# The last up product of a two-layer Flamingo block in three fp32r passes

## The chip, the cores and the metric

The kernel is one program on one core of a Trainium2 chip. The metric is device time in microseconds (us), the median of three timed runs; the rows below come from one further execution that the hardware profiler recorded. TensorE is PE, VectorE is DVE, ScalarE is ACT, GpSimd is POOL, and SP issues DMAs. Each engine works its own queue in order; engines meet only through semaphores.

## What is computed

Two layers over `x` of 16 sequences x 128 rows x 128, each layer a cross attention to a context and a feed-forward part. Layer 0 has 16 heads and a mixture of 16 experts (four chosen per row); layer 1 has one head and a feed-forward part whose hidden size is 512, with butterfly transforms on both sides of the gelu:

```
x = x + tanh(g_xattn[0]) * xattn0(layernorm(x), ctx)
x = x + tanh(g_ffn[0])   * mixture(layernorm(x))
x = x + tanh(g_xattn[1]) * xattn1(layernorm(x), ctx)
x = x + tanh(g_ffn[1])   * ffn1(layernorm(x))
# ffn1
h = einsum('bsd,dh->bsh', x, W_exp) + b_exp
h = butterfly(h, up_weights, 512)
h = gelu(h + up_bias)
h = butterfly(h, down_weights, 512)
y = einsum('bsh,hd->bsd', h, W_con) + b_con + down_bias
```

A butterfly is linear, so the kernel multiplies its 9 stages into the weights once: `W_exp` with the up stages gives `wup` (128 x 512), `W_con` with the down stages gives `wdn`. What is left of `ffn1` per row is an up product with `wup`, a gelu and a down product with `wdn`.

## The kernel before

All engines run one hand-written order; no scheduler decides anything. The 16 sequences go in four groups `g` of 512 rows.

**First 155 us: layer 0's attention.** PE, ACT and DVE work on scores, exponentials and sums. Meanwhile POOL splits the expert weights into a rounded fp32r part and a remainder (L387, L388), then runs the 18 butterfly stages of the weights in `stage` (L424 on). A stage is two 128x512 multiplies (L365, L369), one addition (L373) and a fetch of the next coefficients (L339). Stage 8 (`k == STAGES - 1`) writes `wup`; stages 9 to 17 make the down weights in `bfly`. Between stages POOL has other duties in a fixed place: after stage 9 the second norm of the first half and `norm_rows(0)` (L469, L471), which PE turns at L923 with `turn_normed(0)`; after stage 15 `remainders(0)` (L484), which PE's first expert product waits for. After stage 17 come the up bias, `values1` (L422), `norm2(1)`, and then POOL's `mixture(0)`, whose first piece is `router_ties(1)` (L503, L504). DVE's `router_chosen(1)` (L1301 on) waits for those ties, DVE's next expert work is queued behind it, and PE's `turn_gates(1)` (L937) waits for DVE's gates.

**155 to 350 us: the mixture.** `up(g, e)` is already in the split form: three passes for each of two branches (L994, L995, L996), fp32r, 512 columns. `down(g, e - 3)` is one full fp32 product (L1005). Layer 1's attention of group `g - 1` is strewn among the experts of group `g`. PE is the engine the others wait for in most of it.

**From 350 us: layer 1's feed-forward.** PE turns the normed rows of a group (`turn_rows`, L1028); ACT's `hidden_xt` (L762) copies them from PSUM to `xnts`, and signals `d_xnt`. PE's `hidden_in(g, c)` (L1113) is one full fp32 product for each of four 128-wide slices `c` of the hidden size, ACT's `hidden` (L767) the gelu, and PE's `hidden_out` (L1128) the down product; group 3 is done in half groups (`hidden_half`, L1120 and L773). For group 0 the four `hidden_in` stand between the last three `down` products of the mixture; then `turn_rows(1)` and `turn_mixed(3)` (L1017). DVE's order here is: the last two experts (L1434, L1437, L1442), `attn1_stats(2)` (L1402, L1405), `variances` (L1185 to L1193), `residual2(3)` (L1350, L1353), the statistics and norms of layer 1's attention for group 3 (`attn1_norm`, L1376), `normed(2)` (L1417), and so on to `residual4` (L1425).

`high(g)` and `low(g)` are the two fp32r halves of slot `g % 2` of `xhl`, the tile that holds the mixture's split rows.

Of the kernel before, what the change touches and what calls it, by code (L numbers as in the profile page):

```python
# [7 lines left out]
F32 = mybir.dt.float32  # L8
# [32 lines left out]
def flamingo_layers(nc, a, out):  # L41
# [20 lines left out]
    with ExitStack() as ctx:  # L62
        def sb(name, shape, dt=F32):
            return ctx.enter_context(nc.sbuf_tensor(name, shape, dt))
# [96 lines left out]
        bfx = sb("bfx", [P, HID])  # L161
        ubs = sb("ubs", [HC, 3, P])
        ubx = sb("ubx", [P, 3, HC])
        ubw = sb("ubw", [HC, (STAGES - 2) * 2 * P])
        wup = sb("wup", [P, HID])
        wdn = sb("wdn", [P, HC, D])
        upb = sb("upb", [P, HC])
        kt_flat = kt_row[:, :, :].rearrange("p g t -> p (g t)")
        xns = (xn, rings[:, 0, 1, :].rearrange("p (b d) -> p b d", b=GB))
        xnts = (xnt[:, :], rings[:, 0, 0, :])  # L170
        hid = ([bw[:, c // 2, c % 2 * GT:(c % 2 + 1) * GT] for c in range(HC)],
               [qt_row[:, 0, :], qt_row[:, 1, :], kt_flat[:, 0:GT], kt_flat[:, GT:2 * GT]])
        bcd = sb("bcd", [P, D])
# [10 lines left out]
        def turned_bank(b, gg):  # L184
# [8 lines left out]
            w1_split b1_rdy  # L193
            m_xn m_turned m_xnt m_xh m_xl m_lg_mm m_lgd m_exp m_gf m_g_turned gt_st m_gt m_ha m_hb m_gate0 m_gate1 m_gate2 m_gate3 m_sg m_eb m_eq
            m_ec m_s m_y m_ys m_ys_turned m_x2 c_xn c_turned c_xnt c_q c_qt c_s c_max c_exp c_p_turned c_pt c_pv c_x3
            ln2_var ln2_pow x1_st c_st c_rs x3_st d_rs m_xo m_cmp m_ties d_xn d_bias d_turned d_xnt d_h d_g d_o d_x4 d_out dve_own pool_own bw_ld0 bw_ld1 
            bf_rdy wd_turned wd_rdy us_rdy ub_turned ub_rdy upb_rdy""".split()
        s = {n: sem(n) for n in names}

        CH = (SB[1], SB[3], PQ, SB[2], PO)  # L200
# [6 lines left out]
        def pipelined(eng, body):  # L207

            for g in range(G):
                body(g)  # L210
# [18 lines left out]
        def _(sp):  # L229
# [11 lines left out]
            sp.dma_start(rows[:, :], bass.AP(tensor=v.tensor, offset=v.offset, ap=[[0, P], [1, v.shape[0]]])  # L241
                         ).then_inc(s["ld_small"], 16)
            sp.dma_start(ubs[:, 0, :], a["L1_ffn_b_exp"]).then_inc(s["ld_ub"], 16)
            sp.dma_start(ubw[:, :], a["flies_chunks"]).then_inc(s["ld_ub"], 16)

            def stack_k(g):
                for i in range(HG):
# [63 lines left out]
        def _(pool):  # L311
# [16 lines left out]
            def fetch(n):  # L328

                if n < NQ:  # L330
                    src = a["L0_ffn_w1"][:, 4 * n:4 * n + 4, :, :]
                    dst = bw[:, n % 2, :].rearrange("p (e t c) -> p e t c", e=4, t=2)
                elif n < NQ + 2 * STAGES:
                    v = a["flies"]
                    src = bass.AP(tensor=v.tensor, offset=v.offset + (n - NQ) * 2 * HID, ap=[[0, P], [1, 2 * HID]])
                    dst = bw[:, n % 2, :]
                else:
                    return
                pool.dma_start(dst, src).then_inc(s[f"bw_ld{n % 2}"], 16)  # L339
# [86 lines left out]
            def stage(k, op):  # L426

                n = NQ + k
                w, down = bw[:, n % 2, :], k >= STAGES
                S = 2 ** (2 * STAGES - 1 - k if down else k)  # L430
                if k == STAGES:
                    src = wdn[:, :, :].rearrange("p c d -> p (c d)")
                else:
                    src = bfly[:, (k - STAGES if down else k) % 2, :]
                dst = wup[:, :] if k == STAGES - 1 else bfly[:, ((k - STAGES if down else k) + 1) % 2, :]
                if op == 0:
                    fetched(n)
                    straight(bft[:, :], w[:, 0:HID], src)
                if op == 1:
                    crossed(bfx[:, :], w[:, HID:2 * HID], src, S, HID)  # L440
                if op == 2:
                    summed(dst, bft[:, :], bfx[:, :])
                    fetch(n + 2)

            def norm_scales(stat, mean_, scales, n, both=False):

# [117 lines left out]
        def _(act):  # L564
# [194 lines left out]

            def hidden_xt(g):  # L760
                act.wait_ge(s["d_turned"], g + 1)
                act.activation(xnts[g % 2], (TP if g == 0 else PK)[:, :], ACT.Copy).then_inc(s["d_xnt"], 1)  # L762

            def hidden(g, c):
                need(act, "d_o", g - 1)
# [35 lines left out]
        def _(pe):  # L801
# [305 lines left out]
                        down(g - 1, E - LAG + e)  # L1107

            pipelined(pe, mixture)
            def hidden_in(g, c):  # L1110
                pe.wait_ge(s["d_xnt"], g + 1)
                need(pe, "d_g", g * HC + c - 4)
                pe.matmul(CH[(g * HC + c) % 5][:, :], wup[:, c * P:(c + 1) * P], xnts[g % 2], start=True,  # L1113
                          stop=True).then_inc(s["d_h"], 1)

            def hidden_half(c, i):
                g, t = G - 1, slice(i * GT // 2, (i + 1) * GT // 2)
                pe.wait_ge(s["d_xnt"], g + 1)
                need(pe, "d_g", (g + i) * HC + c - 4)
                pe.matmul(CH[((g + i) * HC + c) % 5][:, t], wup[:, c * P:(c + 1) * P], xnts[g % 2][:, t], start=True,  # L1120
                          stop=True).then_inc(s["d_h"], 1)

            def hidden_out(g, us):
                pe.wait_ge(s["d_g"], (g + 1) * HC + (HC if g == G - 1 and 3 in us else 0))
# [6 lines left out]
                    mm.then_inc(s["d_o"], 1)  # L1131

            every = range(GB)
            pe.wait_ge(s["m_sg"], G * E - 1)
            hidden_in(0, 0)
            down(G - 1, E - 3)
# [37 lines left out]
        def _(dve):  # L1174
# [7 lines left out]
            def variances(n, stat, mean_, both=False, at=0):  # L1182

                c = slice(at, at + n)
                own.mark(dve.tensor_tensor(mean_, stat[:, :, 1], stat[:, :, 4], ALU.add))  # L1185
                own.mark(dve.tensor_tensor(cs[:, 2, 0, c], stat[:, :, 1], stat[:, :, 4], ALU.subtract))
                own.mark(dve.tensor_tensor(cs[:, 3, 0, c], stat[:, :, 2], stat[:, :, 5], ALU.add))
                own.wait()
                own.mark(dve.tensor_scalar(mean_, mean_, 0.5, None, ALU.mult))
                own.mark(dve.tensor_tensor(cs[:, 2, 0, c], cs[:, 2, 0, c], cs[:, 2, 0, c], ALU.mult))  # L1190
                own.mark(dve.tensor_scalar(cs[:, 3, 0, c], cs[:, 3, 0, c], 1.0 / D, EPS, ALU.mult, ALU.add))
                own.wait()
                ins = dve.scalar_tensor_tensor(cs[:, 0, 0, c], cs[:, 2, 0, c], 0.25, cs[:, 3, 0, c],  # L1193
                                               ALU.mult, ALU.add)
                if both:
                    own.then_wait(ins)
                    ins = dve.tensor_scalar(cs[:, 0, 1, c], cs[:, 0, 0, c], 1.0 + EPS, -EPS, ALU.mult, ALU.add)
                ins.then_inc(s["ln2_var"], 1)
# [181 lines left out]
            def attn1_maxima(g):  # L1380
                dve.wait_ge(s["c_s"], g + 1)
                dve.tensor_reduce(mx1[:, :], TP[:, 0:GB * M].rearrange("p (b m) -> p b m", b=GB),
                                  AX.X, ALU.max, negate=True).then_inc(s["c_max"], 1)
# [185 lines left out]
```

## Time and profile before

| | |
|---|---|
| timed runs | 389.17, 392.10, 392.59 us; median 392.1 |
| profiled execution | 395.04 us, of which the span is 393.1 |
| mean granted TensorE clock | 0.912 of full speed |
| PE busy | 324.5 us (83%), 2600 instructions |
| DVE busy | 257.4 us (65%), 602 |
| ACT busy | 209.6 us (53%), 405 |
| POOL busy | 206.9 us (53%), 270 |

Times in the rows are from the span's start. "Busy" is a sum over instructions and says nothing of who waits for whom; that is read from the chain of what ended last and, at each place, from the rows of the engines in order of time. A matmul's printed duration contains its way through the array: what it costs its successors is the distance between starts. A full fp32 product appears as two instructions (x2).

### The profile page before, as it was taken

The page shows a single profiled execution, that of the slowest core. Times are in us where ns is not written, and L with a number is a line of the kernel's source. Part 1 is how long each engine was busy: PE and PEld are TensorE (multiplying, and loading weights), DVE is VectorE, ACT ScalarE, POOL GpSimd, SP SyncE. Part 2 cuts the span into 40 slices and gives each one's busy share as a digit, 9 for nine tenths or more (in the row PEclk, how much of TensorE's full clock was granted, in tenths as well). Part 3 has the DMA queues.
Part 4 walks back from the last instruction along what each step waited for, and adds up shares of the span by engine and source line. Part 5 has one row for each costly group of instructions (what it writes and reads, how often), then busy time and mean ns, then how long its engine had stood idle before and what let it go on. Part 6 is the DMA issues. An engine that isn't in the chain of part 4 may idle for free.

```text
span 393.1 us, 7226 instructions
## 1 busy us (share of the span) xinstructions
PE 324.5 (83%) x2600; PEld 228.2 (58%) x2600; DVE 257.4 (65%) x602; ACT 209.6 (53%) x405; POOL 206.9 (53%) x270
## 2 busy tenths in 40 slices
PE   5758689698799912899199998799998999899986
PEld 2435567576577811666066665566655666555866
DVE  8531436556466287398868789697896887795450
ACT  2642146466366610567145584765866746855543
POOL 7463899979598999999600193002900059122120
PEclk9996759989899755699779999999999999999999
DMA  7669222645531233333133222232322433100001
GB/s 245 129 142 120 86 63 107 133 131 120 112 110 59 69 123 116 128 106 105 29 104 116 80 91 72 85 119 67 105 87 80 119 95 108 53 0 1 28 28 55
DMA packets 17235, 36.66 MB, mean 93 GB/s; under 512 B 2384, under 2 KB 4068, under 8 KB 17064
## 3 DMA queue, kind: packets, MB, share of 16 engines
q1 hardware_dynamic: 13184, 23.53, 21.2%
q0 software_dynamic: 3168, 11.54, 10.8%
q10 hardware_dynamic: 848, 1.14, 0.9%
q8 instruction: 21, 0.34, 0.4%
q14 instruction: 14, 0.11, 0.1%
HBM read 32.79 MB, written 1.18 MB: 86 GB/s over the span
## 4 chain that ended last, share of the span: by engine, by line
PE 36%; POOL 32%; DMA 11%; DVE 7%; issue 6%; ACT 6%; SPq 1%; ACTq 0%; DVEq 0%; POOLq 0%
PE bank L1005 9%; POOL bft L365 6%; POOL bfx L369 5%; POOL bfly L373 5%; PE bank L996 5%; PE bank L994 4%; PE bank L995 4%; DMA bw<-in_L_ffn_w 4%; DMA bw<-in_flies 4%; PE bank L1128 4%; PE bank L1113 3%; DMA x_sb<-in_x 3%; POOL bw L339 2%; POOL w_lo L388 2%; POOL v_all L422 2%
## 5 line engine op out<-in xcount | busy, mean ns | idle before, releaser
L994 PE MATMUL bank<-xhl,w_hi 128*128 128x512 f32 x128 | 76.3, 596 | 0.5 <-ACT rings L734 0.5
L734 ACT ACTIVATE rings<-bank,cols 128x512 f32<-128x512 f32 x64 | 44.1, 689 | 60.9 <-PE bank L996 50.1
L1245 DVE TENSOR_REDUCE nt<-bank 128x4 f32<-128x480 f32 x64 | 39.9, 650 | 46.2 <-PE bank L878 46.2
L1434 DVE SCALAR_TENSOR_TENSOR rings<-rings,gates 128x512 f32<-128x512 f32 x64 | 47.9, 749 | 20.9 <-ACT rings L734 20.5
L996 PE MATMUL bank<-xhl,w_hi 128*128 128x512 f32 x128 | 51.6, 403 | 0.0
L995 PE MATMUL bank<-xhl,w_lo 128*128 128x512 f32 x128 | 51.5, 402 | 0.0
L871 PE MATMUL bank<-rings,ks 32*120 32x128 f32 x512 | 41.7, 306 | 11.4 <-DMA rings<-mxr 6.2
L878 PE MATMUL bank<-ks,rings 32*128 32x120 f32 x512 | 42.9, 312 | 5.8 <-DMA rings<-qt_row 4.0
L871 PEld LDWEIGHTS bank<-rings,ks 32*120 32x120 f32 x512 | 35.2, 201 | 17.4 <-DMA rings<-mxr 8.5
L738 ACT ACTIVATE rings<-bank,b1c 128x512 f32<-128x512 f32 x64 | 44.0, 688 | 1.0 <-PE bank L996 0.6
L878 PEld LDWEIGHTS bank<-ks,rings 32*128 32x128 f32 x512 | 36.5, 213 | 6.6 <-issue 4.2
L994 PEld LDWEIGHTS bank<-xhl,w_hi 128*128 128x128 f32 x128 | 24.8, 194 | 18.8 <-issue 8.4
L995 PEld LDWEIGHTS bank<-xhl,w_lo 128*128 128x128 f32 x128 | 24.9, 194 | 17.5 <-issue 14.4
L484 POOL TENSOR_TENSOR xhl<-xnt,xhl 128x512 fp32r<-128x512 f32 x4 | 5.1, 1270 | 55.5 <-ACT xhl L660 55.4
L1005 PE MATMUL bank<-wide,x_sb 128*128 128x512 f32 x64 | 33.6, 607 | 0.0
L1005 PE MATMUL bank<-rings,x_sb 128*128 128x512 f32 x64 | 33.3, 602 | 0.0
L1437 DVE TENSOR_SCALAR rings<-rings 128x512 f32<-128x512 f32 x64 | 28.9, 452 | 0.7 <-ACT rings L738 0.6
L996 PEld LDWEIGHTS bank<-xhl,w_hi 128*128 128x128 f32 x128 | 24.7, 193 | 5.9
L1442 DVE TENSOR_TENSOR wide<-rings 128x512 f32<-128x512 f32 x32 | 24.0, 749 | 4.2
L1442 DVE TENSOR_TENSOR rings<-rings 128x512 f32<-128x512 f32 x32 | 23.0, 719 | 4.6 <-DVE rings L1437 0.5
L365 POOL TENSOR_TENSOR bft<-bw,bfly 128x512 f32<-128x512 f32 x17 | 21.6, 1272 | 5.4 <-DMA bw<-in_flies 5.1
L937 PE MATMUL bank<-ident,gf 128*16 128x128 f32 x16 | 3.3, 342 | 25.1 <-DVE gf L1315 25.1
(227 smaller groups left out, 688.1 us busy)
## 6 DMA issues: line engine op xcount, KB each, us to landing
gates<-gate_rows SPq DMA_DIRECT2D x64, 256.0 KB, 3.1
bw<-in_flies POOLq DMA_DIRECT2D x18, 512.0 KB, 4.3
bw<-in_L_ffn_w POOLq DMA_DIRECT2D x4, 512.0 KB, 7.8
x_sb<-in_x SPq DMA_DIRECT2D x4, 256.0 KB, 8.3
x_sb<-in_L_ffn_w SPq DMA_DIRECT2D x1, 1024.0 KB, 4.9
wide<-in_ctx ACTq DMA_DIRECT2D x4, 240.0 KB, 7.2
ks<-kt_row SPq DMA_DIRECT2D x16, 60.0 KB
out<-xr SPq DMA_DIRECT2D x3, 256.0 KB, 2.4
```

Of the source, the lines that this page charges most:

```text
L365: own.mark(pool.tensor_tensor(dst, w, src, ALU.mult))
L734: act.activation(esg[:, e % 2, :], SB[1 + e % 2][:, :], ACT.Gelu_apprx_sigmoid, bias=b1_in[:, 0, e:e + 1]).then_inc(s["m_sg"], 1)
L738: act.activation(eb[:, e % 2, :], (SB[3], PK)[e % 2][:, :], ACT.Identity, bias=b1c[:, e:e + 1]).then_inc(s["m_eb"], 1)
L871: mm = pe.matmul(turned_bank(b, gg)[0:M, r * P:(r + 1) * P], ks[32 * gg:32 * gg + 32, i, r, mc], qs[32 * gg:32 * gg + 32, i, r, tc], start ...
L878: mm = pe.matmul(score_bank(ahead, n)[:, r * M:(r + 1) * M], qs[rows32, ia, r, ta], ks[rows32, ia, r, ma], start=True, stop=True)
L994: pe.matmul(bk[:, :], w1_hi[:, e, branch, :], low(g), start=True, stop=False)
L995: pe.matmul(bk[:, :], w1_lo[:, e, branch, :], high(g), start=False, stop=False)
L996: pe.matmul(bk[:, :], w1_hi[:, e, branch, :], high(g), start=False, stop=True).then_inc(s[done], 1)
L1005: pe.matmul(Y[:, :], w2_sb[:, e, :], es[e % len(es)], start=False, stop=(e == E - 1), skip_group_check=True).then_inc(s["m_y"], 1)
L1245: dve.tensor_reduce(nt[:, b % 2, OF[n], :], score_bank(b, n)[:, 0:HR * M].rearrange("p (r m) -> p r m", r=HR), AX.X, ALU.max, negate=True) ...
L1434: dve.scalar_tensor_tensor(eq[:, j, :], esg[:, j, :], GELU_LIMIT, gates[:, (n - 1) % NG, :], ALU.min, ALU.mult).then_inc(s["m_eq"], 1)
L1442: dve.tensor_tensor(es[e % len(es)], eq[:, j, :], ec[:, j, :], ALU.mult).then_inc(s["m_s"], 1)
```

## The change

The up product of `ffn1` takes the form that the mixture's up product has: weights and rows are each split into a rounded fp32r part and a remainder, and three fp32r passes (remainder of the weights by rounded rows, rounded by rounded, rounded by remainder of the rows) add up in PSUM.

```diff
-        ubw = sb("ubw", [HC, (STAGES - 2) * 2 * P])
-        wup = sb("wup", [P, HID])
+        ubw = gates[0:HC, :, :].rearrange("p n t -> p (n t)")[:, 0:(STAGES - 2) * 2 * P]
+        wup_hi = sb("wup_hi", [P, HID], F32R)
+        wup_lo = sb("wup_lo", [P, HID], F32R)
@@ stage (POOL)
-                dst = wup[:, :] if k == STAGES - 1 else bfly[:, ((k - STAGES if down else k) + 1) % 2, :]
+                dst = bfly[:, ((k - STAGES if down else k) + 1) % 2, :]
                 if op == 2:
                     summed(dst, bft[:, :], bfx[:, :])
                     fetch(n + 2)
+                    if k == STAGES - 1:
+                        own.then_wait(pool.tensor_copy(wup_hi[:, :], dst))
+                        pool.tensor_tensor(wup_lo[:, :], dst, wup_hi[:, :].bitcast(F32), ALU.subtract).then_inc(s["wup_rdy"], 1)
+                        pool.wait_ge(s["wup_rdy"], 1)
@@ hidden_xt (ACT)
-                act.activation(xnts[g % 2], (TP if g == 0 else PK)[:, :], ACT.Copy).then_inc(s["d_xnt"], 1)
+                act.activation(high(g), (TP if g == 0 else PK)[:, :], ACT.Copy).then_inc(s["d_xh"], 1)
@@ PE
+            def hidden_product(bk, g, c, t):
+                w = slice(c * P, (c + 1) * P)
+                pe.wait_ge(s["d_xh"], g + 1)
+                pe.matmul(bk[:, t], wup_lo[:, w], high(g)[:, t], start=True, stop=False)
+                pe.matmul(bk[:, t], wup_hi[:, w], high(g)[:, t], start=False, stop=False)
+                pe.wait_ge(s["d_xnt"], g + 1)
+                pe.matmul(bk[:, t], wup_hi[:, w], low(g)[:, t], start=False, stop=True).then_inc(s["d_h"], 1)
@@ DVE
+            def hidden_remainder(g):
+                dve.wait_ge(s["d_xh"], g + 1)
+                dve.tensor_tensor(low(g), (TP if g == 0 else PK)[:, :], high(g).bitcast(F32), ALU.subtract
+                                  ).then_inc(s["d_xnt"], 1)
+
             variances(GB, stats[:, two:three, :], mean[:, two:three], at=GB)
+            hidden_remainder(0)
+            hidden_remainder(1)
             residual2(G - 1)
@@
             residual4(0, every)
+            hidden_remainder(2)
             attn1_maxima(G - 1)
@@
             residual4(2, every)
+            hidden_remainder(3)
             residual4(3, every[:2])
```

`hidden_in` and `hidden_half` call `hidden_product` where they had one matmul. So `d_xnt`, which ACT signalled, is now DVE's signal, and ACT's is `d_xh`. PE also waits once for `wup_rdy` before the tail. `ubw`, the coefficients of the bias stages, now lies in the `gates` tile, which is idle until the mixture.

The order of the instructions, at the places that move. POOL, from stage 8's two multiplies to stage 9's (before):

```order
L365 TENSOR_TENSOR bft<-bw,bfly 128x512
L369 TENSOR_TENSOR bfx<-bw,bfly 128x512
L373 TENSOR_TENSOR wup<-bft,bfx 128x512
L339 DMA bw<-in_flies 128x1024
L365 TENSOR_TENSOR bft<-bw,wdn 128x512
```

and now:

```order
L365 TENSOR_TENSOR bft<-bw,bfly 128x512
L369 TENSOR_TENSOR bfx<-bw,bfly 128x512
L373 TENSOR_TENSOR bfly<-bft,bfx 128x512
L339 DMA bw<-in_flies 128x1024
L445 CAST wup_hi<-bfly 128x512
L446 TENSOR_TENSOR wup_lo<-bfly,wup_hi 128x512
L365 TENSOR_TENSOR bft<-bw,wdn 128x512
```

Two instructions stand in POOL's queue ahead of stage 9 and all that follows it. DVE, from the last expert to `residual2(3)`, before (`cs`, `stats`, `mean` are the variances' tiles):

```order
L1434 SCALAR_TENSOR_TENSOR rings<-rings,gates 128x512
L1437 TENSOR_SCALAR rings<-rings 128x512
L1442 TENSOR_TENSOR wide<-rings 128x512
L1402 COPY gs<-tg 128x1
L1405 BN_STATS stats<-xr 128x6 x4
L1185 TENSOR_TENSOR mean<-stats 128x4
...
L1193 SCALAR_TENSOR_TENSOR cs<-cs 128x4
L1350 TENSOR_TENSOR wide<-wide,bank 128x512
L1353 SCALAR_TENSOR_TENSOR xr<-wide,tg,xr 128x512
```

and now:

```order
L1443 SCALAR_TENSOR_TENSOR rings<-rings,gates 128x512
L1446 TENSOR_SCALAR rings<-rings 128x512
L1451 TENSOR_TENSOR wide<-rings 128x512
L1411 COPY gs<-tg 128x1
L1414 BN_STATS stats<-xr 128x6 x4
L1194 TENSOR_TENSOR mean<-stats 128x4
...
L1202 SCALAR_TENSOR_TENSOR cs<-cs 128x4
L1488 TENSOR_TENSOR xhl<-bank,xhl 128x512 x2
L1359 TENSOR_TENSOR wide<-wide,bank 128x512
L1362 SCALAR_TENSOR_TENSOR xr<-wide,tg,xr 128x512
```

The remainders of groups 0 and 1 stand behind the last expert, the statistics and the variances, and ahead of `residual2(3)`. PE at the end of the mixture, before (L1028 is `turn_rows`, L1005 `down`, L1113 `hidden_in`):

```order
L1028 MATMUL bank<-ident,xn 128x128 x4
L1005 MATMUL bank<-rings,x_sb 128x512
L1113 MATMUL bank<-xnt,wup 128x512
L1005 MATMUL bank<-rings,x_sb 128x512
L1113 MATMUL bank<-xnt,wup 128x512
L1005 MATMUL bank<-wide,x_sb 128x512
```

and now:

```order
L1028 MATMUL bank<-ident,xn 128x128 x4
L1005 MATMUL bank<-rings,x_sb 128x512
L1117 MATMUL bank<-xhl,wup_lo 128x512
L1118 MATMUL bank<-xhl,wup_hi 128x512
L1120 MATMUL bank<-xhl,wup_hi 128x512
L1005 MATMUL bank<-rings,x_sb 128x512
L1117 MATMUL bank<-xhl,wup_lo 128x512
```

Each L1113 row (two instructions on the chip) has become three, of which the last (L1120) waits for DVE, with the mixture's remaining `down` products queued behind it.

## Rows read from the trace of the kernel before

**Rows 1.** The page's chain that ended last: shares of the span by engine
```profile
PE 36%; POOL 32%; DMA 11%; DVE 7%; issue 6%; ACT 6%; SPq 1%; ACTq 0%; DVEq 0%; POOLq 0%
```

**Rows 2.** POOL in order of time: start, duration (us), engine, line, operation, tiles, count, [idle before <-releaser]
```profile
44.60 1.05 POOL L387 CAST w_hi<-bw 128x1024 fp32r<-128x1024 f32 x1
45.73 2.33 POOL L388 TENSOR_TENSOR w_lo<-bw,w_hi 128x1024 fp32r<-128x1024 f32 x1
...
113.32 1.28 POOL L365 TENSOR_TENSOR bft<-bw,wdn 128x512 f32<-128x512 f32 x1
...
125.70 1.04 POOL L471 TENSOR_TENSOR xn<-xn,rr 128x512 f32<-128x512 f32 x1
...
155.25 1.28 POOL L484 TENSOR_TENSOR xhl<-xnt,xhl 128x512 fp32r<-128x512 f32 x1
...
187.57 0.25 POOL L504 TENSOR_TENSOR gw<-gw 128x32 f32<-128x32 f32 x1
```

**Rows 3.** PE in order of time, up to the restart of the mixture
```profile
127.56 0.60 PE L923 MATMUL bank<-ident,xn 128*128 128x128 f32 x4
...
159.90 0.78 PE L994 MATMUL bank<-xhl,w_hi 128*128 128x512 f32 x1
...
186.67 0.40 PE L995 MATMUL bank<-xhl,w_lo 128*128 128x512 f32 x1
186.91 0.40 PE L996 MATMUL bank<-xhl,w_hi 128*128 128x512 f32 x1
195.64 1.02 PE L937 MATMUL bank<-ident,gf 128*16 128x128 f32 x4 [8.34 <-DVE gf L1315]
```

**Rows 4.** DVE in order of time: the router's wait, then the tail
```profile
187.86 0.22 DVE L1301 TENSOR_REDUCE gs<-gw 128x4 f32<-128x64 f32 x1 [2.36 <-POOL gw L504]
...
351.58 0.69 DVE L1442 TENSOR_TENSOR wide<-rings 128x512 f32<-128x512 f32 x1
...
354.03 0.16 DVE L1193 SCALAR_TENSOR_TENSOR cs<-cs 128x4 f32<-128x4 f32 x1
357.56 0.69 DVE L1350 TENSOR_TENSOR wide<-wide,bank 128x512 f32<-128x512 f32 x1 [3.36 <-PE bank L1017]
...
363.98 1.11 DVE L1417 TENSOR_SCALAR xn<-xr,mean,rr 128x128 f32<-128x128 f32 x4
```

**Rows 5.** PE in order of time, in the tail
```profile
350.30 1.10 PE L1113 MATMUL bank<-xnt,wup 128*128 128x512 f32 x2
351.24 1.02 PE L1005 MATMUL bank<-rings,x_sb 128*128 128x512 f32 x2
352.09 1.02 PE L1113 MATMUL bank<-xnt,wup 128*128 128x512 f32 x2
...
356.82 0.60 PE L1017 MATMUL bank<-ident,wide 128*128 128x128 f32 x4
357.76 3.67 PE L1113 MATMUL bank<-rings,wup 128*128 128x512 f32 x8 [0.34 <-ACT rings L762]
...
366.13 1.12 PE L1047 MATMUL bank<-rings,wt 128*128 128x512 f32 x2 [0.25 <-ACT rings L705]
...
382.82 3.72 PE L1120 MATMUL bank<-rings,wup 128*128 128x256 f32 x16 [0.69 <-ACT rings L762]
```

**Rows 6.** ACT in order of time, in the tail
```profile
349.56 0.60 ACT L762 ACTIVATE xnt<-bank 128x512 f32<-128x512 f32 x1 [0.34 <-PE bank L1028]
...
377.12 0.69 ACT L767 ACTIVATE bw<-bank,upb 128x512 f32<-128x512 f32 x1 [0.46 <-PE bank L1113]
```

**Rows 7.** Windows of 1 us: length, busy us of PE, PEld, DVE, ACT, POOL, clock, DMA share, GB/s
```profile
190.00:191.00 1.00, 0.00 (x0) 0.00 (x0) 0.97 (x2) 0.00 (x0) 0.92 (x2) 0.87 0.00 0
191.00:192.00 1.00, 0.00 (x0) 0.00 (x0) 0.96 (x2) 0.00 (x0) 1.00 (x2) 0.50 0.00 0
...
200.00:201.00 1.00, 1.00 (x4) 0.81 (x3) 0.59 (x1) 0.41 (x2) 0.00 (x0) 0.51 0.32 94
201.00:202.00 1.00, 1.00 (x4) 0.47 (x4) 0.41 (x2) 1.00 (x2) 0.00 (x0) 1.00 0.00 0
```

More of the change, by code:

```diff
@@ L169, in flamingo_layers @@
         xns = (xn, rings[:, 0, 1, :].rearrange("p (b d) -> p b d", b=GB))
-        xnts = (xnt[:, :], rings[:, 0, 0, :])
         hid = ([bw[:, c // 2, c % 2 * GT:(c % 2 + 1) * GT] for c in range(HC)],
@@ L195, in flamingo_layers @@
             m_ec m_s m_y m_ys m_ys_turned m_x2 c_xn c_turned c_xnt c_q c_qt c_s c_max c_exp c_p_turned c_pt c_pv c_x3
-            ln2_var ln2_pow x1_st c_st c_rs x3_st d_rs m_xo m_cmp m_ties d_xn d_bias d_turned d_xnt d_h d_g d_o d_x4 d_out dve_own pool_own bw_ld0 bw_ld1
-            bf_rdy wd_turned wd_rdy us_rdy ub_turned ub_rdy upb_rdy""".split()
+            ln2_var ln2_pow x1_st c_st c_rs x3_st d_rs m_xo m_cmp m_ties d_xn d_bias d_turned d_xh d_xnt d_h d_g d_o d_x4 d_out dve_own pool_own bw_ld0 bw_ld1
+            bf_rdy wup_rdy wd_turned wd_rdy us_rdy ub_turned ub_rdy upb_rdy""".split()
         s = {n: sem(n) for n in names}
@@ L243, in _ @@
             sp.dma_start(ubs[:, 0, :], a["L1_ffn_b_exp"]).then_inc(s["ld_ub"], 16)
-            sp.dma_start(ubw[:, :], a["flies_chunks"]).then_inc(s["ld_ub"], 16)
+            sp.dma_start(ubw, a["flies_chunks"]).then_inc(s["ld_ub"], 16)
             def stack_k(g):
@@ L1109, in _ @@
             pipelined(pe, mixture)
+            def hidden_product(bk, g, c, t):
[5 more added lines that the diff above has]
+                pe.matmul(bk[:, t], wup_hi[:, w], low(g)[:, t], start=False, stop=True).then_inc(s["d_h"], 1)
             def hidden_in(g, c):
-                pe.wait_ge(s["d_xnt"], g + 1)
                 need(pe, "d_g", g * HC + c - 4)
-                pe.matmul(CH[(g * HC + c) % 5][:, :], wup[:, c * P:(c + 1) * P], xnts[g % 2], start=True,
-                          stop=True).then_inc(s["d_h"], 1)
+                hidden_product(CH[(g * HC + c) % 5], g, c, slice(0, GT))
             def hidden_half(c, i):
-                g, t = G - 1, slice(i * GT // 2, (i + 1) * GT // 2)
-                pe.wait_ge(s["d_xnt"], g + 1)
+                g = G - 1
                 need(pe, "d_g", (g + i) * HC + c - 4)
-                pe.matmul(CH[((g + i) * HC + c) % 5][:, t], wup[:, c * P:(c + 1) * P], xnts[g % 2][:, t], start=True,
-                          stop=True).then_inc(s["d_h"], 1)
+                hidden_product(CH[((g + i) * HC + c) % 5], g, c, slice(i * GT // 2, (i + 1) * GT // 2))
             def hidden_out(g, us):
@@ L1133, in _ @@
             every = range(GB)
+            pe.wait_ge(s["wup_rdy"], 1)
             pe.wait_ge(s["m_sg"], G * E - 1)
```

## The prediction

> **What bounds the kernel now.** I read the chain that ended last first, because the table of busy shares would mislead: PE is busy 83% of the span, yet the chain is 36% PE and 32% POOL [rows 1]. So POOL, with 53% busy, holds a third of the end time. Then I read each engine in order of time at the two places that the change touches.
>
> The first is POOL's long run. It works without a gap from stage 8 of the butterflies to the ties of the router, whose last piece starts at 187.57. DVE had waited 2.36 us for that piece, and PE, whose last expert pass before it started at 186.91, stood still 8.34 us until 195.64, when DVE's gates came [rows 2 to 4]. Whatever is added to POOL's queue ahead of 187.57 arrives at PE at 195.64. From there on the expert products follow each other on PE almost without idle time, so the delay reaches the end.
>
> The second is the tail from 350 us. There PE goes through `hidden_in` and `down` back to back [rows 5], ACT has its gelus, and DVE is at first late: it finishes the last expert only at 352.2 (351.58 and 0.69) and the variances at 354.03 and 0.16 [rows 4].
>
> **The change part by part.**
>
> *Weights on POOL.* Two instructions are added. For 1024 columns the rounding took 1.05 and the subtraction 2.33 [rows 2]. For 512 columns the same kind of subtraction took 1.28, so 2.33 = fixed + 2 x (1.28 - fixed) gives a fixed part of 0.23. With it the rounding of 512 columns is 0.23 + 0.82/2 = 0.64. Each instruction is followed by a wait on POOL's own semaphore of about 0.08 (45.65 to 45.73). Sum: 0.64 + 1.28 + 0.16 = **2.1 us**, bounded by 0.53 for a rounding of exactly half and 1.05 for one as long as the row: 2.0 to 2.5. The stage's own addition stays, with another target. The fetch is issued before the split, so no transfer gets later. All the rest of POOL's queue moves by 2.1. What waits for it earlier than 187.57? PE turns `xn` at 127.56, and POOL had written it by 126.74 [rows 2, 3]: now 128.8, so PE stops for about 1.3 there. The first expert pass at 159.90 needs the remainder that ended at 156.53; now 158.6, still early. The 1.3 is hidden, since DVE has 2.36 + 2.1 to spare at the ties. So 2.1 goes through to PE's restart.
>
> *The products themselves.* One fp32r pass costs 0.24 (186.67 to 186.91; six passes and a down product fill 2.25 in the mixture), three cost 0.70. A full fp32 product costs 0.86 (351.24 to 352.09) [rows 3, 5]. So 0.16 is saved for each of 12 full-width products, and for the eight half ones, 3.72/8 = 0.465 now, some 0.345 is my estimate (three times 0.115, half a pass), saving 0.12 each. Total at most 12 x 0.16 + 8 x 0.12 = 2.9, if PE sets the end at each.
>
> The Trainium skill (FP8 and Floating Point Precision, section TensorE Precision Notes) counts four passes for true fp32, and TensorE: Matmul & The Clock Gate (section "Wait — 56ns, not 53.3ns?") a full-speed pace of 215.7 ns for 512 columns: four passes against three would save 0.216 a product. That would be 2.6 instead of 1.9 for the twelve, 0.7 us better than my sum. The rows give fp32r passes 0.233 to 0.24 apart, and I go by the rows.
>
> *Rows on ACT.* `hidden_xt` writes `high(g)` instead of `xnts`, the same copy of 512 columns (0.60) [rows 6]. Nothing.
>
> *Rows on DVE: the new wait.* The subtraction reads PSUM and has 512 columns, like the 0.69 of L1350 [rows 4]. For group 0 ACT's copy is ready at 349.56 + 0.60 = 350.16, but DVE reaches the remainder only behind the last expert, the statistics and the variances, at 354.1, and ends it at 354.8. PE used to begin `hidden_in(0, 0)` at 350.30. It now does two passes by 350.77 and then stands until about 354.9; the third ends at 355.15 where the full product had made way at 351.24. **PE is 3.95 late**. Nothing on DVE depends on what is queued behind the third pass until `residual2`, so this is a wait and no deadlock. Queued behind it are three `down` products, `hidden_in(0, 1..3)`, `turn_rows(1)` and `turn_mixed(3)`. Three more `hidden_in` at 0.16 less make `turn_mixed` start at 360.3 instead of 356.82: 3.5 late.
>
> DVE then would begin `residual2` 0.74 after that, at 361.05. But ahead of it stands the remainder of group 1. ACT copies that group's rows after `turn_rows(1)`, from 360.55 to 361.15; the remainder runs 361.2 to 361.9. So `residual2`, 357.56 before, starts at 361.9: **4.35 late**. All of `residual2`, the statistics, `attn1_norm` and `normed(2)` follow it by 4.35. `normed(2)`, which ended at 365.09 (363.98 + 1.11), ends at 369.45 [rows 4]. PE meanwhile: `hidden_in(1)` from 361.3, its first third pass held 0.25 by DVE, four products until 364.4, `hidden_out(0)` until 367.9; it then waits for `attn1_norm` (368.4) and `normed(2)` (369.45). Its chain to `attn1_q`, 366.13 before, waits for ACT's copy and then for the turned rows: it starts at 369.95, **3.8 late** [rows 5]. From there to the softmax of group 3 the order of before repeats, shifted 3.8.
>
> *What comes back.* Group 2's `hidden_in` ends earlier: its last three products save 0.48, and the first lets ACT load its gelu table 0.16 sooner. The last gelu, at 377.12 before after 0.46 of waiting for PE [rows 6], starts about 0.65 sooner. In group 3 the half products start when ACT has copied (382.82 before [rows 5]); the remainder holds the first third pass until 0.78 later, and eight products save 8 x 0.12 = 0.96. With the two passes done meanwhile (0.23), that is 0.25 better. Together 0.9 back.
>
> *Sum for the tail*: 3.8 - 0.9 = **2.9 late**, although PE's own work got shorter. Sum of all: 2.1 + 2.9 = **5.0**. The profiled execution's span of 393.1 becomes 398.1, and its time 395.04 becomes 400.0. It stood 2.9 above the median of the timed runs, 392.1; the same step puts the median at **397.1**.
>
> **The rivals.**
>
> *The clock falls in the new stall (chance 0.25).* In the pause from 187.3 the granted clock went from full, 2.4 GHz, to half, 1.2 GHz, at about 190.9, 3.6 after PE's last work, and was back only at 201.0, 5.4 after PE began again [rows 3, 7]. The new stall is 4.1 us long (350.8 to 354.9), a little more than 3.6. If the clock falls there too and stays for 5.4, the 5.4 hold half the work: 2.7 more, with part of it off the path, so some 2.5. Time: 399.6. It decides if the clock is still at full when the third pass starts. Against it: pauses of 1 to 1.6 us in the mixture left it at full. The Trainium skill warns of just this (TensorE: Matmul & The Clock Gate, section "HAM oscillation — how this bites in real kernels": idle gaps put the clock back down).
>
> *One of the two terms is hidden (0.17).* If POOL's 2.1 were taken up, by DVE or PE work that turns out to bound at 187, or if the restart and half-speed stretch at 195.6 end sooner relative to the restart, only the tail counts: 395.0. If DVE reaches its remainders sooner, or the attention of group 3 has more give than the rows show, the sum is 394 to 395.5. Both are within 1% of before.
>
> *The gain wins (0.06), the other sign.* The mechanism: PE's work in the tail is what ends last, and DVE's remainder comes while PE would be busy anyway. Then 2.9 are gained; with POOL's 2.1 the time is 391.3, and 389.2 if that too is hidden. It needs DVE to deliver group 0's remainder before 350.8; the rows have DVE in the last experts until 352.2 and the remainder behind nine more instructions, which speaks against it. It decides from the point where that third pass waits less than 0.5.
>
> **How the numbers follow.** My forecast, slower by 5.0 at full clock in the tail, has 0.52; the clock rival 0.25; one term hidden 0.17; the gain 0.06. The timed runs of before spread by 3.4, so about 1% (3.9 us) is what this measurement can tell from none. Slower by more than that begins at 396.0: the forecast lies just 1.1 above, and I take three quarters of its 0.52 and nearly all of the clock rival, plus a little, 0.66. Within 1% takes the rest of the forecast and the hidden terms, 0.31, and faster is 0.03. The range runs from 394.2 (one term hidden and a bit of gain) to 400.4 (the clock rival with the upper price of the rounding).
>
> **What would show it.** POOL's row of ties near 189.7 and PE's restart near 197.7, against 187.57 and 195.64, show the first term. An idle time of about 4.1 us on PE ahead of the third pass of the first hidden product, released by DVE, shows the second, and `residual2` 4.3 later than 357.56 (plus 2.1) how it spreads. The granted clock around 355 to 362 (plus 2.1) tells the clock rival. I am wrong if the gap between PE's restart and its `turn_rows(0)` changes, if the third pass is released early, or if passes of 256 columns take much more than 0.115.

## The result and the profile after

The changed kernel takes 397.56 us (median of 8) against 391.4 (median of 8): a ratio of 1.0156, 95% interval 1.0108 to 1.0204. On another chip, later, it was 399.74 against 391.64, ratio 1.0211 (1.0168 to 1.0255). The ratios leave out single executions more than 1.5% above the fastest of their kernel. It is slower, and the time lies where it was forecast, but not for all of the forecast's reasons.

The profiled execution of the changed kernel has a span of 393.5 us, hardly more than the 393.1 of before, at a time (395.54) near the lower end of its own runs. The reason is a part of the program that the change does not touch, so single spans must not be compared whole. I cut each span at three instructions that every variant has: the start of stage 8's addition on POOL (L373), PE's restart after the router (`turn_gates(1)`, 195.64 in [rows 3]), and `turn_rows(0)` on PE. Differences of starts, in us; the tail is what is left to the span, which is printed to a tenth:

| kernel | start to stage 8 | to PE's restart | to turn_rows(0) | tail | span |
|---|---|---|---|---|---|
| before | 111.14 | 84.50 | 153.26 | 44.20 | 393.1 |
| before, second profile | 107.66 | 84.41 | 152.38 | 44.15 | 388.6 |
| changed | 105.16 | **86.52** | 152.20 | **49.62** | 393.5 |
| changed, second profile | 107.61 | **86.43** | 152.56 | **49.80** | 396.4 |

The first column differs by up to 6 us between profiles of code that is the same there: POOL waits, for fetches above all, longer or shorter. The third differs by about 1; that this is how soon the clock is back after the restart is likely, and was not tested. The second and the fourth repeat within 0.2, and there the change stands: 2.0 us more and 5.4 to 5.6 us more, 7.4 to 7.7 in all.

POOL of the changed kernel in order of time (start, duration, engine, line, operation, tiles, [idle before <-releaser]) at the split of the weights and at the ties, which answers to [rows 2]:

```profile
105.16 1.27 POOL L373 TENSOR_TENSOR bfly<-bft,bfx 128x512 f32<-128x512 f32 x1
106.72 0.59 POOL L339 DMA_DIRECT2D bw<-in_flies  x1 [0.30 <-POOL bfly L373]
107.31 0.62 POOL L445 CAST wup_hi<-bfly 128x512 fp32r<-128x512 f32 x1
108.02 1.27 POOL L446 TENSOR_TENSOR wup_lo<-bfly,wup_hi 128x512 fp32r<-128x512 f32 x1
109.37 1.27 POOL L365 TENSOR_TENSOR bft<-bw,wdn 128x512 f32<-128x512 f32 x1
...
183.61 0.25 POOL L508 TENSOR_TENSOR gw<-gw 128x32 f32<-128x32 f32 x1
```

Stage 9 starts 4.21 after stage 8's addition, against 2.18 (113.32 less 111.14, the duration of the row and its fetch included). The rounding took 0.62, the subtraction 1.27; 4.21 less 2.18 is 2.03.

DVE of the changed kernel, from the last expert to `residual2(3)`, which answers to [rows 4]:

```profile
346.56 0.69 DVE L1451 TENSOR_TENSOR wide<-rings 128x512 f32<-128x512 f32 x1
...
349.01 0.16 DVE L1202 SCALAR_TENSOR_TENSOR cs<-cs 128x4 f32<-128x4 f32 x1
349.09 0.68 DVE L1488 TENSOR_TENSOR xhl<-bank,xhl 128x512 fp32r<-128x512 f32 x1
358.70 0.69 DVE L1488 TENSOR_TENSOR xhl<-bank,xhl 128x512 fp32r<-128x512 f32 x1 [8.93 <-ACT xhl L766]
359.31 0.68 DVE L1359 TENSOR_TENSOR wide<-wide,bank 128x512 f32<-128x512 f32 x1
```

and PE of the changed kernel beside it, which answers to [rows 5]:

```profile
343.88 0.63 PE L1032 MATMUL bank<-ident,xn 128*128 128x128 f32 x4 [0.40 <-DVE xr L1405]
...
345.28 0.48 PE L1117 MATMUL bank<-xhl,wup_lo 128*128 128x512 f32 x1
345.60 0.40 PE L1118 MATMUL bank<-xhl,wup_hi 128*128 128x512 f32 x1
349.83 0.79 PE L1120 MATMUL bank<-xhl,wup_hi 128*128 128x512 f32 x1 [3.84 <-DVE xhl L1488]
350.42 1.91 PE L1009 MATMUL bank<-rings,x_sb 128*128 128x512 f32 x2
351.34 1.42 PE L1117 MATMUL bank<-xhl,wup_lo 128*128 128x512 f32 x1
352.56 0.63 PE L1118 MATMUL bank<-xhl,wup_hi 128*128 128x512 f32 x1
```

The wait is where it was said to be: two passes, then 3.84 us until DVE has ended the remainder at 349.77, the third pass 5.95 behind `turn_rows(0)`. And the durations behind it show the second thing: passes follow each other at 0.43 us instead of 0.23. In windows of 1 us (length, busy us of PE, PEld, DVE, ACT, POOL, granted clock, DMA share, GB/s):

```profile
347.00:348.00 1.00, 0.00 (x0) 0.00 (x0) 1.00 (x6) 0.00 (x0) 0.00 (x0) 1.00 0.00 0
348.00:349.00 1.00, 0.00 (x0) 0.00 (x0) 0.73 (x7) 0.00 (x0) 0.00 (x0) 0.71 0.00 0
349.00:350.00 1.00, 0.17 (x1) 0.17 (x2) 0.76 (x2) 0.00 (x0) 0.74 (x1) 0.50 0.02 8
...
354.00:355.00 1.00, 1.00 (x3) 0.34 (x1) 0.00 (x0) 0.34 (x1) 0.00 (x0) 0.50 0.00 0
355.00:356.00 1.00, 1.00 (x5) 0.75 (x4) 0.00 (x0) 0.00 (x0) 0.00 (x0) 0.88 0.00 0
```

The clock fell from 2.4 to 1.2 GHz at about 348.4, 2.4 us after PE's last pass had ended, and was back at about 355.2, 5.4 us after PE had begun again. That is the rival that the prediction gave 0.25.

### The profile page after: what moved, and what is told of

Read it like the earlier page. It is cut to its first block, busy times and chain, and to the rows that moved or that the text cites. A ratio compares the mean times of both kernels' runs of the same rounds, so it can differ in the third digit from the quotient of the medians.

```text
span 393.5 us, 7273 instructions
## 1 busy us (share of the span) xinstructions
PE 323.1 (82%) x2620; PEld 229.6 (58%) x2620; DVE 261.8 (67%) x606; ACT 209.2 (53%) x405; POOL 207.6 (53%) x272
## 4 chain that ended last, share of the span: by engine, by line
POOL 33%; PE 32%; DVE 10%; DMA 9%; ACT 7%; issue 7%; SPq 1%; ACTq 0%; DVEq 0%; POOLq 0%
PE bank L1009 10%; POOL bft L365 6%; POOL bfly L373 5%; POOL bfx L369 5%; PE bank L1000 4%; PE bank L998 4%; PE bank L999 4%; DMA bw<-in_L_ffn_w 3%; DMA bw<-in_flies 3%; PE bank L1136 3%; DMA x_sb<-in_x 3%; POOL bw L339 2%; POOL w_lo L388 2%; DVE rings L1443 2%; POOL pcs L464 2%
## 5 line engine op out<-in xcount | busy, mean ns | idle before, releaser
L882 PE MATMUL bank<-ks,rings 32*128 32x120 f32 x512 | 44.1, 319 | 4.7 <-DMA rings<-qt_row 3.0
L882 PEld LDWEIGHTS bank<-ks,rings 32*128 32x128 f32 x512 | 37.5, 219 | 5.6 <-issue 3.2
L1009 PE MATMUL bank<-wide,x_sb 128*128 128x512 f32 x64 | 34.5, 622 | 0.0
L1009 PE MATMUL bank<-rings,x_sb 128*128 128x512 f32 x64 | 34.5, 621 | 0.0
L1446 DVE TENSOR_SCALAR rings<-rings 128x512 f32<-128x512 f32 x64 | 30.0, 469 | 0.1
L348 POOL TENSOR_TENSOR cs<-cs,minus_half 128x4 f32<-128x4 f32 (+1 forms) x5 | 6.3, 1268 | 39.4 <-DVE cs L1202 39.4
L1451 DVE TENSOR_TENSOR rings<-rings 128x512 f32<-128x512 f32 x32 | 23.0, 719 | 4.6 <-DVE rings L1446 0.5
L1451 DVE TENSOR_TENSOR wide<-rings 128x512 f32<-128x512 f32 x32 | 23.1, 722 | 4.2
L373 POOL TENSOR_TENSOR bfly<-bft,bfx 128x512 f32<-128x512 f32 x18 | 23.2, 1289 | 1.4
```

Source lines behind the costliest of these rows:

```text
L373: own.then_wait(pool.tensor_tensor(dst, a_, b_, ALU.add))
L882: mm = pe.matmul(score_bank(ahead, n)[:, r * M:(r + 1) * M], qs[rows32, ia, r, ta], ks[rows32, ia, r, ma], start=True, stop=True)
L1009: pe.matmul(Y[:, :], w2_sb[:, e, :], es[e % len(es)], start=False, stop=(e == E - 1), skip_group_check=True).then_inc(s["m_y"], 1)
L1451: dve.tensor_tensor(es[e % len(es)], eq[:, j, :], ec[:, j, :], ALU.mult).then_inc(s["m_s"], 1)
```

## The experiments

What had to be told apart: whether POOL's split goes through to the end in full, whether the longer tail is the wait, the clock or the longer queues, and what the three passes are worth alone. The chain that I expected: **split on POOL 2.0, wait behind DVE's queue 2.9 net, clock 2.5**. The rivals stand in the expectations. Every variant's stretches, in the cuts of the table above, with the time against before on the same chip:

| run | to PE's restart | to turn_rows(0) | tail | ratio to before, 95% interval |
|---|---|---|---|---|
| split only | 87.43 | 152.00 | 44.18 | 1.0031 (0.9996 to 1.0066) |
| filler in the stall | 86.58 | 153.35 | 47.12 | 1.0040 (1.0004 to 1.0076) |
| the same, other chip | 86.46 | 153.25 | 47.05 | 1.0110 (1.0072 to 1.0148) |
| early remainder | 87.98 | 152.00 | 43.39 | 0.9995 (0.9963 to 1.0028) |
| no remainder | 86.48 | 153.09 | 41.87 | 0.9963 (0.9933 to 0.9993) |
| late split | 85.81 | 152.13 | 49.55 | 1.0146 (1.0109 to 1.0183) |
| late split, early remainder | 85.68 | 152.30 | 43.41 | 1.0006 (0.9977 to 1.0034) |
| both, quiet place | 84.43 | 153.49 | 43.41 | 1.0030 (0.9981 to 1.0079) |
| residual first | 84.40 | 153.17 | 45.68 | 1.0018 (0.9982 to 1.0055) |

### The split alone

```diff
 # the kernel before, with
                     fetch(n + 2)
+                    if k == STAGES - 1:
+                        own.then_wait(pool.tensor_copy(wup_hi[:, :], dst))
+                        pool.tensor_tensor(wup_lo[:, :], dst, wup_hi[:, :].bitcast(F32), ALU.subtract).then_inc(s["wup_rdy"], 1)
+                        pool.wait_ge(s["wup_rdy"], 1)
```

> The kernel before plus the split of the weights on POOL (rounding and subtraction behind stage 8) and nothing else: the products stay full fp32 and the split parts are read by nobody. Theory (the split lies on POOL's chain, 2.0 to 2.1 us, and goes through to PE's restart after the router): the stretch from the start of stage 8's addition to PE's restart is 86.5 us as in the changed kernel, against 84.5 before; the tail from turn_rows(0) to the end stays at 44.2; time 2 us above before. Rival (the split is hidden behind DVE or PE): the stretch stays at 84.5 and the time at that of before.

The tail is that of before, 44.18, and stage 9 starts 4.21 after stage 8's addition, as in the changed kernel. The stretch to the restart is 87.43, 2.9 to 3.0 longer than before and 0.9 more than expected. In this execution the first expert pass came 54.0 us after stage 8's addition, against 48.7 before, and DVE had only 1.28 us of idle time ahead of the ties, where it had 2.36 before [rows 4]:

```profile
184.52 0.22 DVE L1307 TENSOR_REDUCE gs<-gw 128x4 f32<-128x64 f32 x1 [1.28 <-POOL gw L510]
```

So more expert work of DVE lay beside POOL's norms and ties, and POOL's small pieces took longer there: the first three of the ties took 0.53, 0.47 and 0.67 us, and 0.19, 0.29 and 0.19 in the changed kernel. From the ties to the restart it is 7.84 us, as in the kernel before.

The early remainder's run (below) has the same late first expert (54.0 us) and the longest stretch, 87.98, but it is lost at another place. There the ties were ready at 184.79, 0.7 sooner than in the changed kernel, counted from stage 8's addition. DVE was not: beside POOL's next work its three instructions for an expert took 1.77, 1.26 and 1.31 us instead of 0.69, 0.41 and 0.69, and it came to the ties without any idle time, 4.8 us late:

```profile
185.26 1.77 DVE L1450 SCALAR_TENSOR_TENSOR rings<-rings,gates 128x512 f32<-128x512 f32 x1
186.95 1.26 DVE L1453 TENSOR_SCALAR rings<-rings 128x512 f32<-128x512 f32 x1
188.34 1.31 DVE L1458 TENSOR_TENSOR wide<-rings 128x512 f32<-128x512 f32 x1
```

So in that one execution of thirteen it was DVE, not POOL's ties, that set PE's restart. Why the first expert started late in these two is open.

In time the split alone is 1.0031, an interval that holds zero as well as 2.6 us: the first column's play is larger than the effect, and only the stretches show it.

### Work in the stall

```diff
                 pe.matmul(bk[:, t], wup_hi[:, w], high(g)[:, t], start=False, stop=False)
+                if g == 0 and c == 0:
+                    pe.wait_ge(s["m_eb"], G * E)
+                    for _ in range(14):
+                        pe.matmul(PK[:, :], wup_hi[:, w], high(g), start=True, stop=True)
                 pe.wait_ge(s["d_xnt"], g + 1)
```

> The changed kernel with 14 more fp32r matmuls (512 columns, into a bank that nobody reads then) between the second and the third pass of the first hidden product, some 3.3 us of PE work inside the 3.84 us in which PE stands still. The wait for DVE stays. Theory (of the 5.4 us that the profiled tail is longer, 2.9 are the wait and what it moves, 2.5 the clock that falls to half in it): the clock stays at full, the tail from turn_rows(0) to the end is 47.1 us instead of 49.6. Rival (the clock costs nothing, the whole 5.4 is the wait and the longer queue): the tail stays at 49.6, or grows.

The tail is 47.12 and, in a second profile, 47.05. More work on PE, and a shorter tail. PE in that second profile:

```profile
346.05 0.63 PE L1032 MATMUL bank<-ident,xn 128*128 128x128 f32 x4 [0.41 <-DVE xr L1409]
...
347.99 3.43 PE L1122 MATMUL bank<-xhl,wup_hi 128*128 128x512 f32 x14
352.00 0.50 PE L1124 MATMUL bank<-xhl,wup_hi 128*128 128x512 f32 x1 [0.58 <-DVE xhl L1492]
352.34 1.02 PE L1009 MATMUL bank<-rings,x_sb 128*128 128x512 f32 x2
```

The third pass is released as late as in the changed kernel, 5.95 behind `turn_rows(0)`. Only what follows is quicker, and the window shows why:

```profile
352.00:353.00 1.00, 1.00 (x4) 0.68 (x4) 0.00 (x0) 0.42 (x1) 0.44 (x1) 1.00 0.00 0
```

So the 5.4 us split into 2.9 of waiting and what it moves (47.1 less 44.2) and 2.5 of clock (49.6 less 47.1). The rival, that the clock costs nothing, falls.

For the time this was run again beside the changed kernel:

> The changed kernel unaltered, on the chip of the next three. Theory: stretch from stage 8's addition to PE's restart 86.5 to 88 us (the upper end where the first expert starts late, as in the two runs in which it started 54 us after stage 8's addition), tail 49.6 us with the clock at half in it, or 47.1 in an execution in which the clock stays up; time 1.0 to 1.6% above before.

> The changed kernel with the 14 extra matmuls in PE's stall, timed again beside the changed kernel itself on one chip. Theory (the clock falls in the stall in most executions): some 2 to 2.5 us (0.6%) under the changed kernel; tail 47.1. Rival (it falls only now and then, the profile caught a rare one): within 0.2% of the changed kernel in time, although the tail of the profile is 47.1.

Ratios of 1.0211 and 1.0110 to the same before: 1.0% between them, medians 399.74 and 396.59 (of 6 and 5 executions), 3.15 apart, more than the 2 to 2.5 expected. Stretches of the changed kernel are 86.43 and 49.80, as expected; its time, 2.1% above before, is over the 1.0 to 1.6% expected. In all three profiles in which PE stands 3.8 us at this place (changed, changed again, late split) the clock fell: 2.4, 2.7 and 2.2 us after PE's last pass had ended. Over the timed executions it is only inferred from the 1.0%.

### DVE's place in the queue

```diff
 # DVE, mixture(g)
                 for e in range(E):
                     j, n = e % 2, g * E + e + 1
+                    if e == E - 1 and last(g):
+                        hidden_remainder(0)
 ...
             variances(GB, stats[:, two:three, :], mean[:, two:three], at=GB)
-            hidden_remainder(0)
             hidden_remainder(1)
```

> The changed kernel with DVE's remainder of group 0 moved ahead of the work of the last expert, nothing else. Theory (the stall is DVE's queue, not DVE's work): PE's wait ahead of the third pass shrinks from 3.84 us to under 0.8, the clock stays at full, and the tail is 44 to 45 us instead of 49.6; time 4 to 5 us under the changed kernel's profile, some 2 above before (POOL's split). Rival (DVE is simply too busy there, or the last expert delayed by 0.7 holds down products instead): the tail stays above 47.

```profile
346.81 0.63 PE L1032 MATMUL bank<-ident,xn 128*128 128x128 f32 x4 [0.41 <-DVE xr L1405]
...
348.53 0.40 PE L1118 MATMUL bank<-xhl,wup_hi 128*128 128x512 f32 x1
349.08 0.50 PE L1120 MATMUL bank<-xhl,wup_hi 128*128 128x512 f32 x1 [0.15 <-DVE xhl L1439]
349.87 0.79 PE L1117 MATMUL bank<-xhl,wup_lo 128*128 128x512 f32 x1
```

PE's wait went from 3.84 to 0.15 us, and the tail from 49.6 to 43.39, better than the 44 to 45 expected and 0.8 under before. DVE has the same work; only its place moved by one expert. The whole kernel comes to 0.9995 of before. Some 2 us above before had been expected, for POOL's split; the stretches of this one profile do add up to 1.4 to 2.4 over those of before, by the long first one (87.98) told of above. One line in DVE's order held all that the tail had lost.

### The passes alone

```diff
-                pe.wait_ge(s["d_xnt"], g + 1)
-                pe.matmul(bk[:, t], wup_hi[:, w], low(g)[:, t], start=False, stop=True).then_inc(s["d_h"], 1)
+                pe.matmul(bk[:, t], wup_hi[:, w], high(g)[:, t], start=False, stop=True).then_inc(s["d_h"], 1)
 # and no hidden_remainder; who waited for d_xnt waits for d_xh
```

> The changed kernel without DVE's four remainders: the third pass multiplies the rounded rows once more (so the part of the product with the rows' remainders is left out and the rounded one counted double), three passes as before, and nobody waits for DVE. It prices the three passes alone. Theory: passes of 512 columns follow each other every 0.233 us, of 256 columns every 0.117; the tail is 44.2 minus what PE gets back, 1 to 2.9, so 41.3 to 43.2 us. Rival (ACT's gelus and the softmax chain set the tail, not PE): the tail stays at 44.2.

The tail is 41.87, inside the expected 41.3 to 43.2: the three passes are worth 2.3 us where nobody waits for remainders. So the remainders as they stand in the changed kernel cost 5.2 at full clock (47.1 less 41.9), and with the early remainder still 1.5 (43.4 less 41.9).

### POOL's place in the queue

The split was moved to the start of POOL's `mixture(1)`, behind `rows_again(0)`; stage 8 writes a `wup` of its own again.

```diff
-                    if k == STAGES - 1:
-                        own.then_wait(pool.tensor_copy(wup_hi[:, :], dst))
-                        ...
 # POOL, mixture(g)
                     rows_again(g - 1)
+                    if g == 1:
+                        own.then_wait(pool.tensor_copy(wup_hi[:, :], wup[:, :]))
+                        pool.tensor_tensor(wup_lo[:, :], wup[:, :], wup_hi[:, :].bitcast(F32), ALU.subtract).then_inc(s["wup_rdy"], 1)
```

> The changed kernel with POOL's rounding and subtraction of the weights moved from behind stage 8 to the start of its work for the second expert group, where POOL has nothing else due (stage 8 writes a tile of its own again, which the split reads). Theory (the split's 2.1 us are on POOL's chain only because of where it stands): the stretch from stage 8's addition to PE's restart is back at 84.5 us (up to 85.5), the tail stays at 49.6 or 47.1; time some 2 us under the changed kernel's. Rival (the place does not matter, DVE's work bounds the restart): stretch 86.5, time as the changed kernel's.

> Both cures: the split of the weights moved as in the run before, and DVE's remainder of group 0 moved ahead of the last expert. Theory (the two costs add up, and what is left is the gain of the three passes): stretch 84.5 to 85.5, tail 43.4 against 44.2 before; time 0.3 to 1 us under before, 389 to 392. Rival (the costs are not separate, one hides the other): time still 2 us or more above before.

The ties came 1.9 us sooner, 76.8 after stage 8's addition as before, but the stretches are 85.81 and 85.68, just over the 85.5 at the top: 1.2 to 1.4 is left. The late split alone has a median of 397.55, 2.2 under the changed kernel's, as expected. DVE of the late split, from the ties to the gates, and POOL beside it:

```profile
184.38 0.22 DVE L1310 TENSOR_REDUCE gs<-gw 128x4 f32<-128x64 f32 x1 [3.02 <-POOL gw L505]
...
190.27 0.83 DVE L1446 TENSOR_SCALAR rings<-rings 128x512 f32<-128x512 f32 x1
191.23 1.53 DVE L1451 TENSOR_TENSOR rings<-rings 128x512 f32<-128x512 f32 x1
```

```profile
189.75 1.07 POOL L527 CAST wup_hi<-wup 128x512 fp32r<-128x512 f32 x1
190.89 1.32 POOL L528 TENSOR_TENSOR wup_lo<-wup,wup_hi 128x512 fp32r<-128x512 f32 x1
```

The rounding took 1.07 there and 0.62 in its first place; beside it DVE's two instructions took 0.83 and 1.53. In the kernel before, where POOL had nothing to do at this point, they took:

```profile
193.75 0.41 DVE L1437 TENSOR_SCALAR rings<-rings 128x512 f32<-128x512 f32 x1
194.30 0.69 DVE L1442 TENSOR_TENSOR rings<-rings 128x512 f32<-128x512 f32 x1
```

They hold each other up. The Trainium skill (SBUF — State Buffer, section "Who interferes with whom") says that a VectorE instruction in a two-port mode shares a port pair with GpSimd and one of the two is blocked for the whole of the other's instruction, and that one with two SBUF inputs contends with a GpSimd instruction that reads SBUF. The rows agree in that L1451 reads two SBUF tiles and L528 reads SBUF. With both cures the time is 1.0006 of before (392.68, over the 389 to 392 expected); the rival (one cost hides the other) falls, since each cure acts on its own stretch alone.

So the split went one step further, behind `remainders(2)`, where DVE has no gates due:

> As the run with both cures, but the split of the weights one step later in POOL's queue, behind the remainders of the third expert group, so that it does not run while DVE works out the gates. Theory (while POOL works, DVE's instructions take longer: in the run with both cures the gates came 9.04 us after the ties instead of 7.78): ties to restart 7.8 us again, stretch from stage 8's addition to the restart 84.5, tail 43.4, time 0.8 us under before. Rival (the 1.26 us had another cause): restart still 9.0 us behind the ties.

The restart came 7.8 us behind the ties again, and the stretch is 84.43, that of before; the tail is 43.41. So POOL's work beside the gates was the cause of the 1.2. By stretches this version is 0.7 under before; its time is 1.0030 (0.9981 to 1.0079), its profile having a first column of 111.07. **No version that computes the whole product was shown to beat before in time**: what three passes can still give here is smaller than what this measurement tells. Only the one without remainders, 0.9963 (0.9933 to 0.9993), lies clear below 1.

### The order of the second remainder

The edit is against the version of the row "both, quiet place".

```diff
-            hidden_remainder(1)
             residual2(G - 1)
+            hidden_remainder(1)
```

> The run beside it with DVE's remainder of group 1 behind residual2(3) instead of ahead of it. Theory (both places cost: ahead of it, DVE's chain to normed(2) moves by the remainder; behind it, PE's first third pass of group 1 waits for residual2's two instructions): PE waits some 1.3 us more at that pass, normed(2) comes 0.7 sooner, and the tail is 43.4 to 44.5 us, no better than 43.4. Rival (DVE's chain alone sets the tail): the tail falls to 42.7.

The wait came as expected (1.22 us), the tail did not: 45.68, over the 44.5 at the top. `residual2(3)` started 0.70 sooner, but `normed(2)` only 0.22, and `attn1_q` 2.2 later. PE, and its clock in windows of 2 us:

```profile
355.49 0.40 PE L1118 MATMUL bank<-xhl,wup_hi 128*128 128x512 f32 x1
357.10 0.55 PE L1120 MATMUL bank<-xhl,wup_hi 128*128 128x512 f32 x1 [1.22 <-DVE xhl L1439]
357.46 0.63 PE L1117 MATMUL bank<-xhl,wup_lo 128*128 128x512 f32 x1
357.88 0.63 PE L1118 MATMUL bank<-xhl,wup_hi 128*128 128x512 f32 x1
```

```profile
356.00:358.00 2.00, 0.90 (x3) 0.74 (x4) 1.90 (x8) 0.30 (x1) 0.00 (x0) 0.85 0.00 0
358.00:360.00 2.00, 2.00 (x6) 1.53 (x5) 1.37 (x11) 1.07 (x2) 1.01 (x1) 0.50 0.00 0
```

The clock fell here too, at about 357.4, behind two short pauses of 0.34 and 1.22 us with two passes between them, and was at half for some 3.4 us. That the pauses made it fall is argued from the profile without them, in which it stayed at full here, and was not tested by a filler. The expectation had priced the wait alone. Both places of the remainder cost; ahead of the residual is the cheaper.

### The yardstick

> The kernel before, profiled once more, as the yardstick for the stretches: stage 8's addition to PE's restart 84.5 us, restart to turn_rows(0) 152 to 153.3 (by where the clock comes back), tail 44.2; only the part ahead of stage 8's addition, in which POOL waits for its fetches, differs by some us (111.1 in the first profile of before, 104.9 to 109.2 in the others).

The second and fourth stretches repeated within 0.1. The first was 107.66, 3.5 less than in the first profile of before.

## Why the prediction was right or wrong

*What bounds.* Right: POOL's queue up to the ties is on the path. The split moved the restart by 2.0 and, moved to a quiet place, gave it back. In one execution (early remainder) DVE was the later of the two.

*Split on POOL, 2.1 (2.0 to 2.5).* 2.03 in POOL's rows, 2.0 in the stretch. The rounding by proportion, 0.64, was 0.62. What the sum had no term for is the interference of POOL and DVE, worth 0.9 to 1.5 in four of the variants (split alone, early remainder, and the two with the late split). It is in the kernel before too (one L1442 there took 1.58 us where most take 0.69); what did not show is more of it in the changed kernel than in before.

*Passes.* 0.23 and 0.12 apart, as estimated; the most they can give, 2.9, was put against 2.3 measured, as ACT's copies and the softmax chain take their share.

*The wait.* PE's third pass was put at 6.0 behind `turn_rows(0)` and came at 5.95. (The 3.95 of the prediction is 355.15 less 351.24, which is 3.91; nothing hangs on it.) At full clock (filler) `turn_mixed` is 3.46 late (3.5), `residual2` 4.16 (4.35), `attn1_q` 3.66 (3.8), and 0.8 comes back (0.9). The net of 2.9 was 2.9.

*The clock: the step that failed.* The likeliest case had the clock at full through a pause of 4.1 us, because pauses of 1 to 1.6 had left it there, and gave the fall 0.25. It fell in each of the three profiles with that pause. The size of the rival was right, 2.5 added to the sum; its chance was not. The one fall that I read, in the pause from 187.3, came 3.4 us after the last pass, and I took 3.6 as if it were a threshold that 4.1 only just passes. The falls in the new pause came 2.2 to 2.7 after the last pass, those in the router's pause of all thirteen profiles 2.4 to 3.8, and one came behind pauses of 0.34 and 1.22. The trace of before also held a pause of nearly the new one's length that I had not read, 3.99 us up to 30.54, with the clock at half from 30.3 on:

```profile
30.54 1.85 PE L878 MATMUL bank<-ks,rings 32*128 32x120 f32 x14 [3.99 <-DMA rings<-qt_row]
```

```profile
30.00:31.00 1.00, 0.46 (x4) 0.49 (x6) 0.00 (x0) 0.00 (x0) 1.00 (x1) 0.66 0.96 144
31.00:32.00 1.00, 1.00 (x14) 1.00 (x14) 0.00 (x0) 0.00 (x0) 1.00 (x1) 0.50 1.29 146
```

With the fall the sum is 7.5, and the profiles' stretches say 7.4 to 7.7.

*The total.* The forecast of 397.1 is therefore near the 397.56 partly by luck: the 5.0 were too little by the stretches, and the time differed by 6.2 on the first chip and 8.1 on the second, with a part ahead of stage 8 that plays by up to 6 us in single executions. The first chip's interval (some 4.2 to 8.0 us) holds both 5.0 and 7.5, the second's (6.6 to 10.0) only 7.5. The range's top of 400.4 is more than its parts give: 397.1, 2.5 for the clock and 0.4 for the rounding are 400.0. Of the rivals, hidden terms and the gain fall: both terms are there in full.

## What to carry to other kernels

An operation is as late as its queue: the remainder took 0.7 us, its place behind the last expert and the statistics took 3.8 of PE's time, and moving it by one expert returned all of the tail's loss. When an engine's signal is handed to another engine, read what that other engine is doing at that moment. A new pause on TensorE of nearly 4 us should be priced with the clock as the likely case, since it fell in all three profiles that had one here; a forecast of shorter ones from these rows would be a guess. Some harmless matmuls into a free bank show in one run how much of a loss is clock. And where an untouched part of the program plays by more than the effect, cut the spans at instructions that all variants share.

## What the runs showed that I had not expected

- The granted clock went to half 2.2 to 2.7 us after PE's last pass at one place (three profiles), 2.4 to 3.8 at another (thirteen), and behind two pauses of 0.34 and 1.22 at a third, while other pauses of 1.3 to 1.6 left it at full. It came back 5.1 to 5.7 us after PE had begun again in the tail, and 2.7 to 5.7 at the router.
- A pause is not the whole story. In four of the thirteen profiles the clock was at half for 3.4 us early in the mixture, between 167 and 178. In one of them, the second profile of before, PE had not paused for as much as 0.3 us in the 10 us ahead of it. What made it fall there is open. Its windows:

```profile
167.00:168.00 1.00, 1.00 (x5) 0.34 (x3) 0.90 (x2) 0.14 (x1) 1.00 (x1) 1.00 0.30 115
168.00:169.00 1.00, 1.00 (x4) 0.65 (x3) 1.00 (x2) 0.00 (x0) 1.00 (x2) 0.68 0.38 131
```

- Fourteen extra matmuls of 512 columns made the tail 2.5 us shorter.
- POOL's rounding of 512 columns took 0.62 us in its first place and 1.07 beside DVE's expert work, and DVE's product of two SBUF tiles 1.53 instead of 0.69.
